# Hashed experts: dense columns out of VectorE's turn, rows dealt back by the outputs' store

## The reference, cut to what matters

```
e_idx = token_ids * 5099 % 16                     # 16 experts, 256 rows each
buf[slot] = xk                                    # rows sorted by expert
h = square(relu(expert_in @ w_key))               # 256x512 @ 512x1024, per expert
expert_out = h @ w_value                          # 256x1024 @ 1024x512
y = out_pad[slot]                                 # every token fetches its row back
```

## Time and profile before

| | |
|---|---|
| median of 3 runs | 2496.48 us (2495.56 to 2496.51) |
| the profiled execution | 2494.64 us |
| its span in the profile | 2492.9 us |
| PE busy | 2429.3 us, 97% |
| DVE busy | 1195.2 us, 48% |
| ACT busy | 901.0 us, 36% |

### The profile page before, as it was taken

The page is one execution under the profiler, slowest core; times in us unless marked ns, Lnnn a source line. Parts: engine busy times, 40 slices in busy tenths (PEclk is TensorE's granted clock), DMA queues, the critical chain, the costliest instruction groups (busy, mean ns, idle before and its releaser), DMA issues.

```text
span 2492.9 us, 40630 instructions
## 1 busy us (share of the span) xinstructions
PE 2429.3 (97%) x12307; PEld 2021.7 (81%) x12309; DVE 1195.2 (48%) x1833; ACT 901.0 (36%) x1459; POOL 548.4 (22%) x498
## 2 busy tenths in 40 slices
PE   8999999999999899999999989999999999999999
PEld 4778888888899688888888868888888888888877
DVE  5555455325343243443444357777753333333356
ACT  3233333216555322222222236666652222222234
POOL 1100000002222266666666610000001111111100
PEclk9999999999999899999999999999999999999999
DMA  8698888407466533364345256666642111111135
GB/s 287 203 336 301 304 320 312 164 18 275 164 214 248 178 114 115 109 254 120 106 126 178 93 197 223 235 242 225 233 171 77 51 44 45 51 46 46 42 101 185
DMA packets 165172, 420.68 MB, mean 169 GB/s; under 512 B 31379, under 2 KB 67699, under 8 KB 148578
## 3 DMA queue, kind: packets, MB, share of 16 engines
q1 hardware_dynamic: 137810, 322.08, 37.2%
q0 software_dynamic: 19072, 61.66, 8.1%
q10 hardware_dynamic: 8208, 35.88, 3.8%
HBM read 558.71 MB, written 144.80 MB: 282 GB/s over the span
## 4 chain that ended last, share of the span: by engine, by line
PE 68%; DMA 2%; DVE 2%; issue 2%; ACT 1%; SPq 0%; POOL 0%; another core or an unknown queue 0%; DVEq 0%; POOLq 0%; ACTq 0%
PE s_g L99 8%; PE s_g L101 8%; PE s_g L100 8%; PE s_h_ps L99 5%; PE s_h_ps L101 5%; PE s_h_ps L100 5%; PE s_z_ps L99 2%; PE s_z_ps L101 2%; PE s_z_ps L100 2%; PE s_o_ps L99 2%; PE s_o_ps L100 2%; PE s_o_ps L101 1%; PE s_h L99 1%; PE s_h L100 1%; PE s_h L101 1%
## 5 line engine op out<-in xcount | busy, mean ns | idle before, releaser
L99 PE MATMUL s_g<-wx_hi,s_x_hi 128*128 128x512 f32 x512 | 203.3, 397 | 2.3 <-DVE s_x_lo L2339 1.6
L101 PE MATMUL s_g<-wx_hi,s_x_lo 128*128 128x512 f32 x512 | 199.8, 390 | 0.0
L100 PE MATMUL s_g<-wx_lo,s_x_hi 128*128 128x512 f32 x512 | 199.4, 390 | 0.0
L2234 POOL DMA_INDIRECT s_y<-mid_hash_out,first_rec x32 | 31.5, 985 | 736.0 <-DMA mid_hash_out<-s_o 392.7
L2045 DVE TENSOR_TENSOR s_w_lo<-s_w_raw,s_w_hi 128x1024 fp32r<-128x1024 f32 x124 | 146.4, 1221 | 46.6 <-ACT s_w_hi L1974 45.4
L99 PE MATMUL s_h_ps<-s_x_hi,s_w_hi 128*128 128x256 f32 x512 | 145.7, 285 | 7.1 <-DVE s_x_lo L2077 7.1
L99 PE MATMUL s_g<-s_u,s_c_hi 128*128 128x512 f32 x384 | 150.2, 391 | 1.6 <-PEq L1858 1.6
L101 PE MATMUL s_g<-s_u,s_c_lo 128*128 128x512 f32 x384 | 149.9, 390 | 0.0
L100 PE MATMUL s_g<-s_u,s_c_hi 128*128 128x512 f32 x384 | 149.4, 389 | 0.0
L101 PE MATMUL s_h_ps<-s_x_hi,s_w_lo 128*128 128x256 f32 x512 | 145.5, 284 | 0.0
L100 PE MATMUL s_h_ps<-s_x_lo,s_w_hi 128*128 128x256 f32 x512 | 145.5, 284 | 0.0
(11 more groups left out here) (411 smaller groups left out, 6747.3 us busy)
## 6 DMA issues: line engine op xcount, KB each, us to landing
s_half<-mid_w ACTq DMA_DIRECT2D x124, 2048.0 KB
s_w_raw<-in_w SPq DMA_DIRECT2D x64, 512.0 KB, 6.1
mid_w<-s_x_grp SPq DMA_DIRECT2D x32, 1024.0 KB, 5.8
mid_w<-s_pool_b SPq DMA_DIRECT2D x32, 1024.0 KB, 4.9
s_half<-mid_w SPq DMA_DIRECT2D x32, 1024.0 KB
s_w_raw<-in_w2h SPq DMA_DIRECT2D x16, 2048.0 KB, 9.1
s_w_raw<-in_w1h SPq DMA_DIRECT2D x15, 2048.0 KB, 7.5
mid_routed<-s_o_sb SPq DMA_DIRECT2D x72, 256.0 KB
```

The source lines that it names most:

```text
L99: pe.matmul(out, a_hi, w_hi, start=first, stop=False, skip_group_check=True)
L100: pe.matmul(out, a_hi, w_lo, start=False, stop=False, skip_group_check=True)
L101: return pe.matmul(out, a_lo, w_hi, start=False, stop=last, skip_group_check=True)
L2234: pool.indirect_dma_start(y[:], None, d["hash_out"], bass.IndirectOffsetOnAxis(rec[:, SLOTH:SLOTH + 1].bitcast(U32), 0)).then_inc(S["y_in" ...
```

## The change

In `stage_hashed` the turn writes row 4t + s to column 32s + t, so that each transposed block lands in 32 consecutive elements. The outputs of TensorE then have row 4t + s on partition 32s + t, and the store's DRAM side is written as `s t c`: four groups of 32 rows, each row 4 rows behind the one before it. `stage_recurrent` keeps the old turn under a new name.

```diff
+def dealt(rows):
+
+    return rows.rearrange("(t s) c -> s t c", s=4)
...
+def turn_dealt_quarters(dve, dst, src):
+
+    return dve.transpose(dst.rearrange("p k (t s) -> p k s t", s=4), src.rearrange("p (s k a) -> p k s a", s=4, a=32))
...
 def turn_quarters(dve, dst, src):
 
-    return dve.transpose(dst.rearrange("p k (t s) -> p k s t", s=4), src.rearrange("p (s k a) -> p k s a", s=4, a=32))
+    return dve.transpose(dst.rearrange("p k (s t) -> p k s t", t=32), src.rearrange("p (s k a) -> p k s a", s=4, a=32))
...
                     sp.wait_ge(S[f"o_ready{m}"], e + 1)
-                    sp.dma_start(d["hash_out"][bass.ds(e * CAP + m * P, P)], o_sb[m][:]).then_inc(S[f"o_out{m}"], 16)
+                    sp.dma_start(dealt(d["hash_out"][bass.ds(e * CAP + m * P, P)]), o_sb[m][:]).then_inc(S[f"o_out{m}"], 16)
...
-                turn_quarters(dve, tx_ps[:], y[:]).then_inc(S["tx"], 1)
+                turn_dealt_quarters(dve, tx_ps[:], y[:]).then_inc(S["tx"], 1)
```

## The result

The changed kernel takes 2512.8 us in the median of 4 runs (2509.8 to 2513.7) against 2496.48: ratio 1.0064, 95% interval 1.0047 to 1.0082. I had forecast 2489.4, faster. It is 16 us slower, and outside my range.

A forecast was written before the change was run, and what follows sets the result against it. PE was taken as the bound (97% busy), stalled by VectorE's turns. From the profiled 2494.64 us, -10.1 - 0.4 + 1.5 + 2.0 = -7.0 gave 2487.6, or 2489.4 for the median; range 2485.0 to 2496.5.

The forecast's parts named there:

- The bound and the turn: Hashed loop: PE stalls 0.71 us at 15 low parts behind VectorE's turns; turns fall from 1091 to 680 ns, gaining 10.1 us.
- The store on a quarter of the engines: Output stores in the hashed stage: outermost dimension 4 puts them on 4 DMA engines, the same ones the row loads use.
- The store's duration: Each output store of 262 KB, 0.60 to 0.80 us before, gets 1.6 to 2.4 us longer; 2.0 taken.
- (a): Inside the loop: four engines need 20.9 to 22.1 of 22.62 us per expert; second row load still meets its turn, cost 0.
- The second rival: Loop: the four engines fill, rows land late, VectorE holds h_lo(3) behind the waiting turn; 2505.6 us, chance 0.1.
- (b): Last expert: load_ahead queues behind the last but one store(1), delaying ScalarE and so PE; +1.5 us once, bounds 0 to 2.4.
- (c): Stage end: the last store lands later, delaying the fetch and PE's first turn behind it; +2.0 us, bounds 0 to 2.4.
- The first expert: Loop start: PE waits 7.1 us for x_lo; the faster second turn in that chain gains 0.4 us once.

The follow-up runs named there:

- store0_dealt: Changed kernel with only store(1) cut into four DMAs of 32 partitions, store(0) left as one DMA; 2505.79 us, ratio 1.0043.
- four_loads: Changed kernel, both stores still single DMAs, with each row load cut into four DMAs by quarter of the columns; 2490.37 us, ratio 0.9980.
- blocks_store: Changed kernel with stores of four groups whose 32 rows lie side by side in DRAM (rows in wrong order); 2512.56 us, ratio 1.0065.
- dense_plain: Changed kernel with the plain store of before, so the dense turn alone (rows in wrong order); 2486.58 us, ratio 0.9962.
- store0_behind: Changed kernel with store(0) issued a round later, behind the next row loads and ahead of store(1), except the last expert's; 2493.32 us, ratio 0.9988.
- strided_dealt: Kernel before, strided turn kept, with only the store changed to the four-group form (rows in wrong order); 2518.37 us, ratio 1.0088.
- store1_dealt: Changed kernel with only store(0) cut into four DMAs of 32 partitions, store(1) left as one DMA; 2492.76 us, ratio 0.9991.
- last_dealt: Changed kernel with every store cut into four DMAs except the last expert's, which stay single; 2490.93 us, ratio 0.9979.
- four_stores: Changed kernel with each store cut into four DMAs, one per group of 32 partitions; 2488.57 us, ratio 0.9971.
- four_both: Changed kernel with each store cut into four DMAs by 32 partitions and each row load into four by column quarter; 2487.45 us, ratio 0.9961.

## Why the prediction was wrong, step by step

Against the forecast of the sum (-10.1 in the loop, -0.4 at the first expert, +3.5 at the end) the profiled executions give +8.7, +2.4 and +7.9.

- **The bound and the turn: right.** Turns of 708 ns (I took 680, with 718 beside it), a pair in 1.30 us. The loop alone came to 22.75 us where I had 22.62, and the turn alone to 2486.6: a gain of 10.3 by the medians, where I had 10.1 + 0.4.
- **The store on a quarter of the engines: right.** Share 0.25. The rule of the Trainium skill that I quoted ("DMA: Bandwidth & Descriptors", section "Why a DMA increments its semaphore by 16 and not by 1") is borne out in both directions: an outermost 4 gives a quarter, with dealt rows or with blocks, and 32 on both sides gives the full gain back. Which of the engines they were, no view of the profile shows; that store and row loads share them is argued from store0_dealt and four_loads.
- **The store's duration: the mis-sized term.** "Each store gets 1.6 to 2.4 us longer; I take 2.0." It is 3.8 to 4.2 us against 0.8, so 3.0 to 3.4 longer. I took the rates of loads in mid-flight, 87 and 109 GB/s; the store reaches 104 but begins at 30, and has no time to make up for it. The last store, behind the one before, landed after 5.92 us (blocks_store), +3.9 instead of +2.0.
- **The step that failed by it: (a), the deadline of the second row load.** "Rows land 15.2 to 16.5 after; the turn is due at 16.9 ... Spare 0.4 to 1.7 us: cost 0." They landed 18.0 after (1596.99 to 1615.01), the loop being already held up. (The terms in my brackets give 16.8 and not 16.9, which changes nothing.) The spare time was smaller than the error of one term, and I should have priced the far end rather than set it to 0. With 3.4 in place of 2.0 my own sum gives up to 17.9. The cost that I set at 0 was 1.21 us per expert, the period of 23.96 against dense_plain's 22.75, and that alone turned the forecast gain into a loss.
- **The second rival: the right outcome by half the right mechanism.** It named the late rows, the waiting turn and `h_lo(3)` behind it, and the point "stores at 70 GB/s or less"; I held that for 1 in 10. But it tied the price to the engines' throughput ("once the queue of these engines needs more than 23.33 us"). With stores of 3.8 to 4.2 us my sum of (a) comes to 23.7 to 24.5 us per expert, and the period was 23.96; that agreement is luck, for store0_behind has the same work and a period of 22.71. The runs show a circle instead: turn, `x_lo`, `w1`'s low part, next `w1` load, and ahead of it `store(0)`, then the rows, then the turn. strided_dealt lengthens it by the turn, store0_behind opens it at the same throughput.
- **(b) and (c), the end: the mis-sized term again, and a path that was wrong.** Forecast +3.5, measured +7.9. For (b), 1.5, ScalarE's wait grew by 2.8 and PE's waits behind it by 2.4. For (c) I let the last store and the fetch alone set PE's first turn, "Nothing covers it". In the changed kernel PE didn't wait for the fetched rows there. Two links were missing in my text: SP holds the step between stages until `store(0)` has landed (PE waits 3.85 us there, and 2.1 in store1_dealt, where `store(0)` alone is spread), and PE's granted clock was 0.50 after that wait, which made the 2.7. The fetch is close behind, at some 1.5: in store1_dealt, with a short step and the full clock, PE did wait 3.6 us for it.
- **The first expert:** +2.4 where I had -0.4. The mark scatters by 5 us between profiled executions, more than either, so what made it late here is open.

## What to carry to other kernels

When a store's or load's access pattern is rewritten to save engine time, look at the outermost dimension of both sides first: here 4 in place of 128 made the same 256 KB about five times as slow, and four DMAs of 32 rows each brought it back (2488.6 us for 2512.8) at 1.25 us more of SP's issue time. Then ask what stands behind that DMA in its queue and whether the producer of the DMA waits for it; a slow store ahead of the loads closed a circle here, and behind them it cost the loop nothing. And a deadline with a spare time below the error of its estimate is a coin toss, not a cost of 0.

## What the runs showed of the hardware that I had not expected

A store over a quarter of the engines starts slowly: 29, 31, 82, 104 GB/s in its first four microseconds, while the row loads on as many engines run at 87. The last stores of blocks_store (31, 29, 88, 100) and store1_dealt (27, 25, 72, 100) do the same. The turn with 16-byte steps costs 1091 ns in SBUF and 718 in PSUM, the dense one 708 in SBUF; a dense turn into PSUM wasn't run.

PE's wait at the step between stages went with the clock of the products behind it. Seven profiled executions waited 3.85 to 4.03 us there (the changed kernel, strided_dealt, store0_dealt, store0_behind, four_loads, last_dealt, blocks_store), and in all of them matmuls then came every 0.43 us for a while, in last_dealt after two at the full pace. Three waited 1.63 to 2.06 us (before, dense_plain, store1_dealt) and kept 0.23. The two between, four_stores with 3.00 and four_both with 3.01, differ: the first kept its pace, the second ran its first six at 0.43.
